# Softmax attention: two fp32r parts in 64-row tiles instead of six bf16 parts over the whole array

## The chip, the cores and the metric

The kernel is one program on one NeuronCore of a Trainium2 chip. The metric is the device time of one execution, in microseconds (us). Engines are named as in the profile: PE (TensorE matmul), PEld (its weight loads), DVE (VectorE), ACT (ScalarE), POOL (GpSimd), SP (the engine that issues the DMAs here).

## The reference

Two macaron blocks are computed on x of 2 x 2048 x 256 in fp32. Block 0 is a routed feed-forward, a causal linear attention and the feed-forward again; block 1 is an fp4-quantised feed-forward, a softmax attention and the quantised feed-forward again. The change touches only the softmax attention:

```python
b, n, _ = x.shape                       # 2, 2048
qkv = (x @ W_qkv.T).reshape(b, n, 16, 16).transpose(0, 2, 1, 3)
score = softmax(einsum('bhif,bhjf->bhij', qkv, qkv) / 4.0, axis=-1)
attn = einsum('bhij,bhjf->bihf', score, qkv)
out = attn.reshape(b, n, 256) @ W_o.T
```

Queries, keys and values are the same tensor: 16 heads of 16 features, 2048 x 2048 scores for each of 2 x 16 heads.

## The kernel before

The stage is `attn1()`. It works in 32 **units**: batch (2) x group of four heads (`NG` = 4) x block of 512 queries (`IC` = 4). A unit has two kinds of big work, both over 512 columns at a time (`GW` = 512):

- **maxima** ("max", 64 in a unit): 128 queries (stationary) against 512 keys (moving) of one head; DVE reduces the PSUM bank to one maximum for each query (line 1817). After 64 of them a small reduce makes the row maxima, PE transposes them ("extremes"), DVE and POOL split them into parts, and two DMAs bring them through DRAM into extra rows of the query operand, negated, so that the score product subtracts them by itself.
- **scores** ("score"): 128 keys (stationary) against 512 queries (moving), for each of 16 key tiles `jt` and four heads. ACT takes the exponential out of PSUM into `spr` (line 1775). Then "pv" multiplies the four heads' probabilities with the values (plain fp32, four 32-column tiles at once, line 1713) into one bank that accumulates over the 16 key tiles. "end" copies that bank to SBUF on ACT, "tail" transposes and divides by the row sums, "ao" and "wo" are the output projection and the residual.

The fp32 precision of the scores comes from **parts**: the projected values are split into three bf16 parts (ACT rounds, DVE takes the rest, POOL rounds and takes the rest again), stored in `q_parts` in DRAM, and gathered into stacks: `KS` holds the parts `KEY = [0,0,1,0,1,2]`, `QS` the parts `QRY = [0,1,0,2,1,0]`, 16 rows each, so that one product over 96 rows is the sum of six partial products; scores use 99 rows (three more for the maxima, against rows of ones in `KS`).

The order of the work is one written-out generator, `plan()`, which every engine walks through; each engine's instructions run in that order. The maxima run 80 ahead of the scores (a unit and a quarter). For each key tile before, the order is: max, two scores, max, two scores, max, pv, max. A pair of scores fills a two-bank PSUM tile that one 1024-wide exponential reads; there are two such tiles, three single banks (`spare`) shared by maxima and all other products in turn, and one bank for pv. The projection of the second batch ("norm", "turn", "parts", "value") and the output steps are put in between, one at a time. A stack for the next group of heads is loaded by SP a group ahead. An `Event` counts a semaphore; `made(what)` is the product being ready, `read(what)` its bank being free.

Of the kernel before, what the change touches and what calls it, by code (L numbers as in the profile page):

```python
# [6 lines left out]
F32 = mybir.dt.float32  # L7
# [7 lines left out]
P = 128  # L15
# [41 lines left out]
def build_program(nc, A):  # L57
# [21 lines left out]
    with ExitStack() as ctx:  # L79
# [1412 lines left out]
        def attn1():  # L1492
            with ExitStack() as scope:
                NPT = 6
                KR = NPT * DH
                KM = KR + 3
                HG = 4
                NG = NH // HG
# [5 lines left out]
                SPU = TB * HG // 2  # L1504
# [3 lines left out]
                PART, REST = ring(scope, "spart", [P, 3, GW], 2, BF16), sb("srest", [P, GW], scope=scope)  # L1508
# [4 lines left out]
                MR, MB = sb("smr", [NR, P], scope=scope), ring(scope, "smb", [NR, 3, P], 2, BF16)  # L1513
                RD, AO = ring(scope, "srd", [P, GT, HG], 2), sb("sao", [P, TB, D], scope=scope)
                AOT = ring(scope, "saoT", [P, D], 2)
                parts = nc.dram_tensor("q_parts", [3, D, L * nb], BF16).ap()
                maxima = nc.dram_tensor("row_maxima", [UNITS, 3, NR, P], BF16).ap()
# [7 lines left out]
                pm_in, pm_free = event("a1_pm_in"), [event(f"a1_pm_free{i}") for i in range(3)]  # L1525
                xn_ok, part0, rest_ok, part_ok = (event(f"a1_{n}") for n in ("xn", "part0", "rest", "part"))
                mx_ok, mb_ok, fill_ok = event("a1_mx"), event("a1_mb"), event("a1_fill")
# [13 lines left out]
                def output_steps(u):  # L1541
                    b, ic = u // (NG * IC), u % IC
                    for t in range(ic * GT, (ic + 1) * GT):
                        yield ("ao", b, t)
                        yield ("wo", b, t)

                def plan():
# [9 lines left out]
                    for u in range(UNITS):  # L1557
# [9 lines left out]
                        for h in range(2 * SPU):  # L1567
                            if m % MPU == 0 and m <= UNITS * MPU:
                                yield ("extremes", m // MPU - 1)
                            if m < UNITS * MPU:  # L1570
                                yield ("max", m)
                            m += 1
                            if h > 9 and h % 4 == 3:
                                yield from itertools.islice(aside, 1)
                            if h > 9 and h % 6 == 4:
                                yield from itertools.islice(put, 1)
                            if h % 4 < 2:
                                yield ("score", u * SPU + h // 4 * 2 + h % 4)
                            if h % 4 == 2 and u * TB + h // 4:
                                yield ("pv", u * TB + h // 4 - 1)  # L1580
                            if h == 2 and u:
                                yield ("end", u - 1)
                            if h == 8 and u:
                                yield ("tail", u - 1)
# [11 lines left out]
                def bank(key):  # L1596
                    return spare[use[key] % 3]

                def read(key):

                    return pm_free[use[key] % 3](use[key] // 3 + 1)
# [4 lines left out]
                with nc.Block() as block:  # L1606

                    @block.sync
                    def _(e):
                        for kind, *at in plan():  # L1610
                            if kind == "parts":
                                b, g, o = at
                                col = b * L + g * GW
                                e.wait_ge(*part_ok((b * IC + g) * KD + o + 1))
                                e.dma_start(parts[:, o * P:(o + 1) * P, col:col + GW].rearrange("s p n -> p s n"),
                                            PART[o][:]).then_inc(*part_out[o].up)
                            if kind == "stack":
# [6 lines left out]
                                for dst, which in ((KS[n % 2], KEY), (QS[n % 2], QRY)):  # L1624
                                    for j, part in enumerate(which):
                                        src = parts[part, g * HG * DH:(g + 1) * HG * DH, b * L:(b + 1) * L]
                                        e.dma_start(dst[j * DH:(j + 1) * DH], src.rearrange(
                                            "(h f) n -> f h n", f=DH)).then_inc(*stack_in[n % 2].up)
                            if kind == "extremes":
                                u = at[0]  # L1630
                                ic, n = u % IC, u // IC
                                e.wait_ge(*mb_ok(u + 1))
                                e.dma_start(maxima[u].rearrange("j r n -> r j n"), MB[u % 2][:]).then_inc(
                                    *max_in[u % 2].up)
                                e.wait_ge(*max_in[u % 2](2 * (u // 2) + 1))
                                e.dma_start(QS[n % 2][KR:KM, :, ic * GW:(ic + 1) * GW],
                                            maxima[u].rearrange("j (h i) n -> j h (i n)", h=HG)).then_inc(
                                    *max_in[u % 2].up)

                    @block.tensor  # L1640
                    def _(e):
                        def free(key):
                            k = use[key]
                            if k >= 3:
                                e.wait_ge(*pm_free[k % 3](k // 3))

                        for what in plan():
# [24 lines left out]
                            if kind == "max":  # L1672
                                u, r = divmod(at[0], MPU)
                                h, i, jc = r // (GT * IC), r // IC % GT, r % IC
                                n, q0 = u // IC, (u % IC * GT + i) * P
                                if r == 0 and u % IC == 0:
                                    e.wait_ge(*stack_in[n % 2]((n // 2 + 1) * 2 * NPT))
# [9 lines left out]
                            if kind == "score":  # L1687
                                q = at[0]
                                u, jt, hp = q // SPU, q % SPU // 2, q % 2
                                n, ic = u // IC, u % IC  # L1690
                                if q % SPU == 0:
                                    e.wait_ge(*max_in[u % 2](2 * (u // 2) + 2))
                                if q == 0:
                                    e.wait_ge(*fill_ok(2))
                                if q >= 2:
                                    e.wait_ge(*exp_ok(q - 1))
                                for i in range(2):
                                    m = e.matmul(st[q % 2][:, i, :], KS[n % 2][0:KM, 2 * hp + i, jt * P:(jt + 1) * P],  # L1698
                                                 QS[n % 2][0:KM, 2 * hp + i, ic * GW:(ic + 1) * GW], start=True,
                                                 stop=True)  # L1700
                                m.then_inc(*st_ok.up)
                            if kind == "pv":
# [7 lines left out]
                                e.wait_ge(*exp_ok(2 * j + 2))  # L1710
# [30 lines left out]
                    def _(e):  # L1741
                        e.wait_ge(*stats_ok(0))
                        std_of(e, 0, T).then_inc(*std_ok.up)
                        e.wait_ge(*fill_ok(2))
# [180 lines left out]
```

## Time and profile before

| | |
|---|---|
| median of 3 runs | 3826.54 us (3825.26 to 3828.68) |
| the profiled execution: its time | 3830.56 us |
| its span, first to last instruction | 3828.8 us |
| PE, PEld busy | 3580.0 us (94%), 2285.8 us (60%) |
| DVE, ACT, POOL busy | 2719.0 us (71%), 2054.4 us (54%), 663.9 us (17%) |
| mean granted TensorE clock | 0.971 |

The busy shares are means over stages that have different limits. The stage of the change lies between about 1840 and 3554 us of the span. A matmul's busy time is counted from its start to its modelled end, and matmuls overlap, so the distance between starts says more than the mean duration. In a timeline row the figures are start, duration, engine, line, operation, output and inputs, and a count; in square brackets the idle time of the engine ahead of it and what ended it.

### The profile page before, as it was taken

How to read it: one execution, taken by the hardware profiler on the slowest of the kernel's cores; microseconds unless marked ns; L12 is line 12 of the kernel's file. 1: busy time of each engine (PE TensorE's matmuls, PEld its weight loads, DVE VectorE, ACT ScalarE, POOL GpSimd, SP SyncE). 2: the span in 40 equal slices, each digit the busy share in tenths (PEclk: the TensorE clock that was granted, in tenths of full speed). 3: DMA queues.
4: the chain of work that ended last, by engine and by line, in shares of the span. 5: the costliest groups of instructions: out<-in, count | busy, mean ns of one | idle time of the engine just before them, and what ended most of it. 6: DMA issues, size and time to landing. Idle time of an engine off the chain costs nothing. (4 is left out here: it accounts for less than half of the span.)

```text
span 3828.8 us, 57043 instructions
## 1 busy us (share of the span) xinstructions
PE 3580.0 (94%) x22274; PEld 2285.8 (60%) x22274; DVE 2719.0 (71%) x4907; ACT 2054.4 (54%) x2806; POOL 663.9 (17%) x601
## 2 busy tenths in 40 slices
PE   6999998999799999799589999999999999999799
PEld 6888886777688888799313333333333333333698
DVE  4545544875444544799378788888888888884898
ACT  3444443433444444455226666666666666667555
POOL 4000002443400000455300000000000000000565
PEclk9999998999899999899869999999999999999899
DMA  3000001000200000000240120202020202000000
GB/s 115 1 1 1 1 1 40 2 2 1 71 1 1 1 1 1 1 1 1 50 50 10 30 31 5 30 9 27 1 34 1 34 2 34 1 1 1 6 18 23
DMA packets 39651, 61.42 MB, mean 16 GB/s; under 512 B 5284, under 2 KB 29912, under 8 KB 39384
## 3 DMA queue, kind: packets, MB, share of 16 engines
q1 hardware_dynamic: 39384, 57.78, 8.3%
q8 instruction: 177, 2.90, 0.3%
q14 instruction: 90, 0.74, 0.1%
HBM read 46.89 MB, written 10.88 MB: 15 GB/s over the span
## 5 line engine op out<-in xcount | busy, mean ns | idle before, releaser
L1817 DVE TENSOR_REDUCE smxp<-psum 128x1 f32<-128x512 f32 x2048 | 1281.7, 682 | 222.8 <-PE psum L1679 222.1
L1775 ACT ACTIVATE spr<-psum 128x1024 f32<-128x1024 f32 x1024 | 996.3, 1021 | 560.1 <-PE psum L1698 557.7
L1679 PE MATMUL psum<-sks,sqs 96*128 96x512 bf16 x2048 | 731.5, 392 | 34.3 <-DMA sqs<-q_parts 31.3
L1698 PE MATMUL psum<-sqs,sks 99*128 99x512 bf16 x2048 | 610.9, 380 | 0.4
L1713 PE MATMUL psum<-spr,sv 128*32 128x512 f32 x4096 | 546.4, 605 | 0.6 <-ACT spr L1775 0.6
L1679 PEld LDWEIGHTS psum<-sks,sqs 96*128 96x128 bf16 x2048 | 164.2, 97 | 614.0 <-issue 379.9
L1698 PEld LDWEIGHTS psum<-sqs,sks 99*128 99x128 bf16 x2048 | 199.7, 98 | 243.2 <-ACT spr L1775 15.2
L1886 POOL CAST smb<-smr 16x128 bf16<-16x128 f32 x32 | 9.0, 281 | 1356.4 <-DVE smr L1836 1356.4
L389 PE MATMUL psum<-w2hi_a,hsa_hi 128*128 128x256 f32 x768 | 217.3, 283 | 17.4 <-DVE hsa_lo L531 17.4
L389 PE MATMUL psum<-w2hi_b,hsb_hi 128*128 128x256 f32 x768 | 217.3, 283 | 10.5 <-DVE hsb_lo L531 10.5
L389 PE MATMUL psum<-w2lo_a,hsa_hi 128*128 128x256 f32 x768 | 217.7, 284 | 0.0
L389 PE MATMUL psum<-w2lo_b,hsb_hi 128*128 128x256 f32 x768 | 217.7, 284 | 0.0
L389 PE MATMUL psum<-w2hi_a,hsa_lo 128*128 128x256 f32 x768 | 217.4, 283 | 0.0
L389 PE MATMUL psum<-w2hi_b,hsb_lo 128*128 128x256 f32 x768 | 217.4, 283 | 0.0
L525 DVE TENSOR_TENSOR hidb<-psum,maskb 128x512 f32<-128x512 f32 x128 | 88.3, 690 | 173.8 <-PE psum L355 173.8
L531 DVE TENSOR_TENSOR hsa_lo<-hida,hsa_hi 128x512 fp32r<-128x512 f32 x192 | 148.0, 772 | 83.6 <-ACT hida L444 75.3
L531 DVE TENSOR_TENSOR hsb_lo<-hidb,hsb_hi 128x512 fp32r<-128x512 f32 x192 | 147.4, 769 | 83.6 <-ACT hidb L444 75.3
L1713 PEld LDWEIGHTS psum<-spr,sv 128*32 128x32 f32 x4096 | 80.7, 108 | 210.7 <-issue 193.3
L525 DVE TENSOR_TENSOR hida<-psum,maska 128x512 f32<-128x512 f32 x128 | 88.2, 689 | 157.5 <-PE psum L355 157.5
L447 ACT ACTIVATE hsb_hi<-hidb,b_b 128x512 fp32r<-128x512 f32 x128 | 92.6, 723 | 183.7 <-DVE hidb L525 183.7
L447 ACT ACTIVATE hsa_hi<-hida,b_a 128x512 fp32r<-128x512 f32 x128 | 92.6, 724 | 173.6 <-DVE hida L525 173.6
L389 PEld LDWEIGHTS psum<-w2hi_a,hsa_hi 128*128 128x128 f32 x768 | 146.0, 190 | 28.8 <-DVE hsa_lo L531 21.1
(350 smaller groups left out, 7259.3 us busy)
## 6 DMA issues: line engine op xcount, KB each, us to landing
sks<-q_parts SPq DMA_DIRECT2D x48, 256.0 KB, 8.8
sqs<-q_parts SPq DMA_DIRECT2D x48, 256.0 KB, 19.7
q_parts<-spart SPq DMA_DIRECT2D x16, 384.0 KB, 2.6
x<-in_L_attn_x_dram SPq DMA_DIRECT2D x8, 512.0 KB, 7.2
rawa<-in_L_ffn_w_dram SPq DMA_DIRECT2D x16, 256.0 KB
rawb<-in_L_ffn_w_dram SPq DMA_DIRECT2D x16, 256.0 KB
out_dram<-x SPq DMA_DIRECT2D x8, 512.0 KB, 2.9
rawa<-in_L_ffn_sw_dram SPq DMA_DIRECT2D x8, 256.0 KB
```

The source lines that it names most:

```text
L389: m = e.matmul(ops[:, i // 2, (i % 2) * D:(i % 2 + 1) * D], hs[u][:, i * P:(i + 1) * P], w2[v][:, ex, c, :], start=(s == 0 and i % 2 == 0 ...
L447: e.activation(hi[:], hid[:], ACT.Relu, bias=bias).then_inc(*sc.up())
L525: e.tensor_tensor(HB[n % 2][:], psum[:, j % 3, :], mask[:, s // C0 - 1, :], ALU.mult).then_inc(*masked.up)
L531: e.tensor_tensor(lo[:], HB[n % 2][:], hi[:].bitcast(F32), ALU.subtract).then_inc(*low_ok.up)
L1679: e.matmul(bank(what), QS[n % 2][0:KR, h, q0:q0 + P], KS[n % 2][0:KR, h, jc * GW:(jc + 1) * GW], start=True, stop=True).then_inc(*pm_in.up)
L1698: m = e.matmul(st[q % 2][:, i, :], KS[n % 2][0:KM, 2 * hp + i, jt * P:(jt + 1) * P], QS[n % 2][0:KM, 2 * hp + i, ic * GW:(ic + 1) * GW], s ...
L1713: m = e.matmul(po[32 * hq:32 * hq + VW, :], VB[b][:, jt, c0:c0 + VW], PR[j % 2][:, hq, :], start=(jt == 0), stop=(jt == TB - 1), tile_posi ...
L1775: e.activation(PR[j % 2][:, 2 * hp:2 * hp + 2, :], st[hp], ACT.Exp, scale=float(DH) ** -0.5).then_inc(*exp_ok.up)
L1817: e.tensor_reduce(MXP[u % 2][:, r // IC, r % IC:r % IC + 1], bank(what), AX.X, ALU.max).then_inc(*pm_free[use[what] % 3].up)
L1886: e.tensor_copy(MB[u % 2][:, 1, :], MR[:]).then_inc(*pl.up())
```

## The change

- Two fp32r parts take the place of three bf16 parts. A stack is then 3 x 16 = 48 rows (`KEY = [0,0,1]`, `QRY = [0,1,0]`), 50 rows with the maxima (in two parts). POOL's casts and subtractions go; DVE writes the second part itself.
- Two heads share the 128 partitions: one in rows 0 to 49, one in rows 64 to 113. Each max and score product is a 64-row tile (`tile_position=(64 * a, 0)`), with `a` alternating 0, 1. Columns, outputs and the number of products stay as they are.
- The PSUM banks are dealt anew: four single banks for the maxima and the small products, three single banks for scores, one for pv. Each score has its own 512-wide exponential (2048 instead of 1024).
- The order for each key tile is `m s0 s1 m s2 v m s3 m`: max, scores 0 and 1, max, score 2, pv of the key tile before, max, score 3, max. A score waits for the exponential three scores back.
- The rows of ones in `KS` are written by eight small DMAs from a 2 x 64 tile, instead of two POOL memsets over 3 x 8192 elements.
- The parts go through DRAM in fp32 (512 KB for each store instead of 384 KB); a stack is still 12 DMAs of 256 KB, six to each of `KS` and `QS`. The maxima come back in two DMAs instead of one.

```diff
-                NPT = 6
+                NPT = 3
                 KR = NPT * DH
-                KM = KR + 3
+                KM = KR + 2
+                HALF = 64
-                KEY = [0, 0, 1, 0, 1, 2]
-                QRY = [0, 1, 0, 2, 1, 0]
+                KEY = [0, 0, 1]
+                QRY = [0, 1, 0]
+                ORDER = ("m s0 s1 m s2 v m s3 m").split()
-                KS, QS = ring(scope, "sks", [P, HG, L], 2, BF16), ring(scope, "sqs", [P, HG, L], 2, BF16)
+                KS, QS = ring(scope, "sks", [P, NPR, L], 2, F32R), ring(scope, "sqs", [P, NPR, L], 2, F32R)
-                st = (psum[:, 0:2, :], psum[:, 2:4, :])
-                po = psum[:, 6, :]
-                spare = (psum[:, 4, :], psum[:, 5, :], psum[:, 7, :])
+                spare = [psum[:, i, :] for i in range(4)]
+                st = [psum[:, 4 + i, :] for i in range(3)]
+                po = psum[:, 7, :]
...
-                        for h in range(2 * SPU):
+                        for jt in range(TB):
+                            j = u * TB + jt
+                            for step in ORDER:
+                                if step[0] == "s":
+                                    yield ("score", j, int(step[1]))
+                                if step == "v" and j:
+                                    yield ("pv", j - 1)
+                                if step == "m":
+                                    if m % MPU == 0 and m <= UNITS * MPU:
+                                        yield ("extremes", m // MPU - 1)
+                                    if m < UNITS * MPU:
+                                        yield ("max", m)
+                                    m += 1
...
                             if kind == "max":
-                                e.matmul(bank(what), QS[n % 2][0:KR, h, q0:q0 + P],
-                                         KS[n % 2][0:KR, h, jc * GW:(jc + 1) * GW], start=True,
-                                         stop=True).then_inc(*pm_in.up)
+                                rows = slice(HALF * a, HALF * a + KR)
+                                e.matmul(bank(what), QS[n % 2][rows, pr, q0:q0 + P],
+                                         KS[n % 2][rows, pr, jc * GW:(jc + 1) * GW], start=True, stop=True,
+                                         tile_position=(HALF * a, 0)).then_inc(*pm_in.up)
...
                             if kind == "score":
-                                if q >= 2:
-                                    e.wait_ge(*exp_ok(q - 1))
-                                for i in range(2):
-                                    m = e.matmul(st[q % 2][:, i, :], KS[n % 2][0:KM, 2 * hp + i, jt * P:(jt + 1) * P],
-                                                 QS[n % 2][0:KM, 2 * hp + i, ic * GW:(ic + 1) * GW], start=True,
-                                                 stop=True)
-                                m.then_inc(*st_ok.up)
+                                if s >= 3:
+                                    e.wait_ge(*exp_ok(s - 2))
+                                e.matmul(st[s % 3], KS[n % 2][rows, pr, jt * P:(jt + 1) * P],
+                                         QS[n % 2][rows, pr, ic * GW:(ic + 1) * GW], start=True, stop=True,
+                                         tile_position=(HALF * a, 0)).then_inc(*st_ok.up)
...
-                                e.wait_ge(*exp_ok(2 * j + 2))
+                                e.wait_ge(*exp_ok((j + 1) * HG))
...
-                        e.memset(KS[0][KR:KM], 1.0).then_inc(*fill_ok.up)
-                        e.wait_ge(*fill_ok(1))
-                        e.memset(KS[1][KR:KM], 1.0).then_inc(*fill_ok.up)
-                        e.wait_ge(*fill_ok(2))
+                        e.tensor_scalar(ones[:], ident[0:2, 0:1].to_broadcast([2, HALF]), 0.0, 1.0, ALU.mult,
+                                        ALU.add).then_inc(*fill_ok.up)
```

## Rows read from the trace of the kernel before

**Rows 1.** Groups: line, engine, shapes, count | busy us, mean ns | idle before.

```profile
L1817 DVE TENSOR_REDUCE smxp<-psum 128x1 f32<-128x512 f32 x2048 | 1281.7, 682 | 222.8 <-PE psum L1679 222.1
L1775 ACT ACTIVATE spr<-psum 128x1024 f32<-128x1024 f32 x1024 | 996.3, 1021 | 560.1 <-PE psum L1698 557.7
L1713 PE MATMUL psum<-spr,sv 128*32 128x512 f32 x4096 | 546.4, 605 | 0.6 <-ACT spr L1775 0.6
L870 PEld LDWEIGHTS psum<-aqe,aqT 32*128 32x128 f32 x512 | 45.2, 189 | 16.2 <-issue 8.7 <-POOL aqe L1178 1.2
```

**Rows 2.** Windows: length, busy PE, PEld, DVE, ACT, POOL, then PEclk, DMA share, GB/s.

```profile
1930.00:1978.50 48.50, 47.06 (x82) 8.32 (x81) 47.65 (x82) 0.00 (x0) 0.70 (x2) 0.50 0.10 14
1978.50:3493.30 1514.80, 1483.21 (x8282) 480.31 (x8282) 1299.49 (x2213) 997.90 (x1078) 34.94 (x76) 1.00 0.13 18
```

**Rows 3.** Timeline of one key tile in the steady state.

```profile
2502.55 0.11 PEld L1679 LDWEIGHTS psum<-sks,sqs 96*128 96x128 bf16 x2 [0.84 <-issue]
...
2502.99 2.48 DVE L1817 TENSOR_REDUCE smxp<-psum 128x1 f32<-128x512 f32 x4 [0.35 <-PE psum L1679]
...
2503.63 1.94 ACT L1775 ACTIVATE spr<-psum 128x1024 f32<-128x1024 f32 x2 [0.90 <-PE psum L1698]
...
2504.39 0.16 PEld L1713 LDWEIGHTS psum<-spr,sv 128*32 128x32 f32 x8 [0.42 <-issue]
...
2505.39 0.11 PEld L1679 LDWEIGHTS psum<-sks,sqs 96*128 96x128 bf16 x2 [0.84 <-issue]
```

**Rows 4.** Timeline where DVE alone sets the pace, with the first extremes.

```profile
1964.40 4.26 DVE L1817 TENSOR_REDUCE smxp<-psum 128x1 f32<-128x512 f32 x7
...
1969.91 0.67 DVE L1817 TENSOR_REDUCE smxp<-psum 128x1 f32<-128x512 f32 x1
```

**Rows 5.** Timeline of PE's weight loads over a key tile with extremes.

```profile
2015.95 0.10 PEld L1679 LDWEIGHTS psum<-sks,sqs 96*128 96x128 bf16 x1 [0.84 <-issue]
...
2020.10 0.11 PEld L1679 LDWEIGHTS psum<-sks,sqs 96*128 96x128 bf16 x2 [0.84 <-issue]
```

**Rows 6.** Timeline of PE: fp32r products over 512 columns in block 0's attention.

```profile
701.12 0.40 PE L760 MATMUL psum<-wqkv0T_hi,axT_lo 128*128 128x512 f32 x1
701.35 0.40 PE L760 MATMUL psum<-wqkv0T_hi,axT_hi 128*128 128x512 f32 x1
```

**Rows 7.** Timeline: plain fp32 products, first in 32-row tiles, then over the whole array.

```profile
702.85 0.52 PEld L870 LDWEIGHTS psum<-aqe,aqT 32*128 32x128 f32 x6
702.85 0.70 PE L870 MATMUL psum<-aqe,aqT 32*128 32x256 f32 x4
...
1890.30 3.70 PE L1662 MATMUL psum<-sxT,wqkv1T 128*128 128x512 f32 x8 [0.47 <-ACT sxT L1753]
```

**Rows 8.** Timeline of the last unit, which has scores and no maxima.

```profile
3501.47 3.91 ACT L1775 ACTIVATE spr<-psum 128x1024 f32<-128x1024 f32 x4 [0.27 <-PE psum L1698]
3501.79 0.16 PEld L1713 LDWEIGHTS psum<-spr,sv 128*32 128x32 f32 x8 [0.42 <-issue]
...
3503.46 0.11 PEld L1698 LDWEIGHTS psum<-sqs,sks 99*128 99x128 bf16 x2 [0.56 <-ACT spr L1775]
3504.00 0.16 PEld L1713 LDWEIGHTS psum<-spr,sv 128*32 128x32 f32 x8 [0.42 <-issue]
...
3504.99 0.11 PEld L1698 LDWEIGHTS psum<-sqs,sks 99*128 99x128 bf16 x2 [0.84 <-ACT spr L1775]
...
3505.26 0.60 ACT L1782 ACTIVATE sot<-psum 128x512 f32<-128x512 f32 x1
```

**Rows 9.** Timeline of the stage's start, up to the first maxima.

```profile
1841.75 6.92 POOL L1868 MEMSET sks<- 3x8192 bf16 x1
...
1855.72 0.39 ACT L1753 ACTIVATE sxT<-psum 128x256 f32<-128x256 f32 x1 [13.85 <-POOL sks L1870]
...
1895.65 0.69 DVE L1810 TENSOR_TENSOR srest<-psum,spart 128x512 f32<-128x512 f32 x1 [2.02 <-POOL spart L1879]
...
1929.66 0.13 PEld L1679 LDWEIGHTS psum<-sks,sqs 96*128 96x128 bf16 x2 [31.67 <-DMA sqs<-q_parts]
```

More of the change, by code:

```diff
@@ L1566, in plan @@
                         put = output_steps(u - 1) if u and (u - 1) // IC % NG == NG - 1 else iter(())
-                        for h in range(2 * SPU):
[L1568 to L1573, printed above, removed]
+                        for jt in range(TB):
[11 more added lines that the diff above has]
+                                    m += 1
+                            if jt == 0 and u:
+                                yield ("end", u - 1)
+                            if jt == 1 and u:
+                                yield ("tail", u - 1)
+                            if jt > 0:
                                 yield from itertools.islice(aside, 1)
-                            if h > 9 and h % 6 == 4:
+                            if jt > 1:
                                 yield from itertools.islice(put, 1)
[L1577 to L1584, printed above, removed]
                         yield from put
@@ L1609, in _ @@
                     def _(e):
-                        for kind, *at in plan():
+                        e.wait_ge(*fill_ok(1))
+                        for ks in KS:
+                            for pr in range(NPR):
+                                for i in range(2):
+                                    e.dma_start(ks[HALF * i + KR:HALF * i + KM, pr, :].bitcast(F32).rearrange("p (c n) -> p c n", n=HALF),
+                                                ones[:].bitcast(F32).unsqueeze(1).to_broadcast([2, L // HALF, HALF])).then_inc(*ones_in.up)
+                        for what in plan():
+                            kind, *at = what
                             if kind == "parts":
@@ L1625, in _ @@
                                     for j, part in enumerate(which):
-                                        src = parts[part, g * HG * DH:(g + 1) * HG * DH, b * L:(b + 1) * L]
-                                        e.dma_start(dst[j * DH:(j + 1) * DH], src.rearrange(
-                                            "(h f) n -> f h n", f=DH)).then_inc(*stack_in[n % 2].up)
+                                        src = parts[part, g * HG * DH:(g + 1) * HG * DH, b * L:(b + 1) * L].rearrange(
+                                            "(r i f) n -> i f r n", i=2, f=DH)
+                                        for i in range(2):
+                                            row = HALF * i + j * DH
+                                            e.dma_start(dst[row:row + DH].bitcast(F32), src[i]).then_inc(*stack_in[n % 2].up)
                             if kind == "extremes":
@@ L1754, in _ @@
                                              bank(what)[:, 0:D].rearrange("p (k n) -> p k n", k=KD),
-                                             ACT.Copy).then_inc(*pm_free[use[what] % 3].up)
+                                             ACT.Copy).then_inc(*pm_free[use[what] % 4].up)
                             if kind == "parts":
@@ L1816, in _ @@
                                     e.wait_ge(*mx_ok(u - 1))
-                                e.tensor_reduce(MXP[u % 2][:, r // IC, r % IC:r % IC + 1], bank(what), AX.X,
-                                                ALU.max).then_inc(*pm_free[use[what] % 3].up)
+                                out = MXP[u % 2][:].rearrange("p (r a i) c -> p r i c a", r=NPR, a=2)
+                                e.tensor_reduce(out[:, r // (2 * GT * IC), r // (2 * IC) % GT, r // 2 % IC, r % 2:r % 2 + 1],
+                                                bank(what), AX.X, ALU.max).then_inc(*pm_free[use[what] % 4].up)
                                 if r == MPU - 1:
-                                    for k in range(3):
+                                    for k in range(4):
                                         e.wait_ge(*read(("max", at[0] - k)))
```

120 lines of the change are left out of this document (52 added, 68 removed).

## The prediction

> **What bounds the kernel now.** I read the windows first. The stage has a stretch with maxima alone and one of 1514.8 us with maxima and scores together [rows 2]. In the second, PE's busy time is 1483 us, but durations overlap there, so it doesn't tell the bound; DVE is busy 1299 us and ACT 998 us, so neither is full. The groups say who waits for whom: DVE's reduces wait 222 us for the max products, ACT's exponentials 558 us for the scores, pv waits for nobody [rows 1]. Both consumers wait for PE. The timeline of one key tile confirms it: the tile repeats every 2505.39 - 2502.55 = 2.84 us. Of this, eight 512-column products (four maxima, four scores) take 2504.39 - 2502.55 = 1.84 us, 0.22 us each with about 0.1 us ahead of pv, and pv takes 1.00 us. PE is never idle; DVE has 2.48 us of reduces and waits 0.35 us, ACT has 1.94 us [rows 3].
>
> By the plan, 2048 - 80 = 1968 maxima lie in this stretch, 4 to a key tile, so 492 key tiles. 492 x 2.835 = 1395 us, and 120 us are left for all else: the extremes (a key tile with them takes 2020.10 - 2015.95 = 4.15 us, 1.31 more, so 31 x 1.31 = 41 us [rows 5]), the second batch's projection, tails and output products.
>
> **What a key tile costs after: PE.** The products are as many and as wide. Two things change. First the rate: fp32r products over 512 columns start 0.235 us apart [rows 6] against 0.22 for bf16. Second, neighbours in different row halves can run at once. No row shows this for fp32r in 64-row tiles. The nearest is block 0's attention: plain fp32 products of 256 columns in two 32-row tiles in turn start about 0.11 us apart: four in 0.70 us, the last of them 0.38 long [rows 7] (a plain fp32 record of 512 columns lasts 0.605 [rows 1], one of 256 by half the columns 0.22 less). Over the whole array the same kind needs (3.70 - 0.60)/7 = 0.44 us for 512 columns [rows 7], so 0.22 for 256. Two row tiles do halve the time there, and the weight loads of 128 fp32 columns keep up: each lasts 0.19 us [rows 1], but six take 0.52, so they start (0.52 - 0.19)/5 = 0.07 us apart [rows 7]. In the new order every product finds a neighbour of the other half: after pv, m2|s3, m3|m0, s0|s1, m1|s2. Four slots of 0.235, plus the 0.1 ahead of pv and pv itself, make 2.04 us. Bounds: all pairs, 2.04; no pairs, 8 x 0.235 + 1.10 = 2.98. I take all pairs, since the one row with row tiles shows the full factor.
>
> The Trainium skill (TensorEngine Tiling, Key Properties) says that changing the tiling mode, not just the tile, drains TensorE. This speaks for a cost at each switch between 64-row products and pv; the rows show such a cost already, since pv is column-tiled before too, about 0.1 us ahead of it and 0.15 inside its 1.00, and the count of switches stays. By the page the sum is then unchanged.
>
> **DVE.** Its reduce is untouched. Back to back, reduces start (4.26 - 0.68)/6 = 0.597 us apart [rows 4], 2.39 us for four. **ACT.** A 1024-wide exponential takes 1.02 us and a 512-wide copy 0.60 [rows 1, 8], so 512 columns cost 0.42 and the rest is fixed; two in a row take 1.94 us, so starts are 0.92 apart; at half the width 0.50, and four make 2.0 us. Neither PE nor ACT nor, at 2.39, DVE needs the old 2.84.
>
> **The chain between PE and ACT.** The new order closes a loop. Score 2 of a key tile reuses the bank of score 3 of the tile before, so it waits for that exponential (e3), as does the pv behind it. Score 3 is issued only after this pv, and e3 follows it. One turn is one key tile:
> - e3's end to the weight load of s2: the second of four exponentials, which start (3.91 - 1.02)/3 = 0.96 apart, ends at 3501.47 + 0.96 + 1.02 = 3503.45, load at 3503.46: 0.01 [rows 8].
> - s2 to pv: 0.54 for two bf16 scores [rows 8], less one at 0.22, plus 0.02 for the rate and 0.08 for an fp32 load of 0.19 [rows 1] instead of 0.11: 0.42.
> - pv to the next load: 0.99 [rows 8].
> - m2 and s3, to the start of e3: a max's load to its reader took 0.44 [rows 3]; plus 0.10 as above, plus 0.06 because s3's load comes second: 0.60.
> - e3: 0.60 [rows 8].
>
> Sum 2.62 us. It is more than PE's 2.04, ACT's 2.0 and DVE's 2.39, so this wait, new with the change, takes the place of the old bound. Lower bound 2.50 (loads hidden, s3 not behind m2), upper 2.75 (m2 and s3 one after the other, 0.14 more). I take 2.62. The maxima's four banks hold 4 x 0.6 us of work for DVE and bridge pv.
>
> **The rest of that stretch.** Extremes: PE stands until DVE has read the last max and the small reduce, then 1969.91 - (1964.40 + 4.26) = 1.25 us go by until its next max, with the small reduce and the copies in them [rows 4]; with m3 read later in the tile I get 1.6 instead of 1.31 us, +10 us over 31 units. The PE work put in between (projection, output products) now falls partly into PE's idle 0.4 us per tile: some 75 such steps that held the path, at most 0.45 each, so up to -34, and DVE's own part of the output steps takes some back: -28. The 120 become 102. Stretch: 492 x 2.62 + 102 = 1391 us, **-124**.
>
> **The stage's start.** Two POOL memsets of 6.9 us hold back ACT's first copy: it waits 13.85 us and starts at 1855.72 [rows 9]. Without them POOL is done at 1841.75 plus a tiny operation; norm and transposes are then the chain and the copy starts near 1843.3: -12. In the projection DVE waits 2.02 us for POOL once a block [rows 9], and PE's value products wait behind it about 1.0: -4 over four blocks; the last parts reach DRAM without POOL's two operations (about the 2 us that DVE waited for them) and without part of that wait: -3; stores are a third larger: +0.6. The stack's load, 31 us ahead of the first max [rows 9], has the same number of DMAs and bytes: 0, with 5 less and 10 more as bounds since its pieces are longer. The eight DMAs of ones are needed only at the first score, 80 maxima (48 us) later: hidden; if not, a few us once. The extremes' second DMA has 16 maxima (9.6 us) of cover. Sum **-18**. The 48.5 us with maxima alone [rows 2] are DVE's and stay.
>
> **The last unit** has no maxima: a key tile from pv to pv takes 3504.00 - 3501.79 = 2.2 us [rows 8]; the loop without m2 is 2.5: 16 x 0.3 = **+5**.
>
> Sum: -124 - 18 + 5 = -137 us on the profiled execution (time 3830.6, span 3828.8), which lies 4 us over the median. From the median 3826.5: **3690 us**.
>
> **The rivals.**
> - *DVE becomes the bound* (the loop closes faster, or its load and latency terms are smaller): 2.39 a tile, 492 x -0.445 = -219, start -18, last unit +3, the 120 stay: 3592. For it: five small terms make up the loop, and each is a bound from bf16 rows. Against: DVE must then never wait. The Trainium skill (TensorEngine Tiling, PSUM Bottleneck) says that tiling speeds up TensorE but not the reading of PSUM; by that rule alone this rival is the answer, and the loop is what I set against it. Chance 0.17.
> - *Pairs overlap only in part* (a pair in about 0.35 us, or waits for banks break pairs up): 2.8 a tile, with the other terms about 3780. Chance 0.10.
> - *No pairs, slower:* fp32r row tiles run one after another. PE again is the bound with 2.98 a tile: 492 x +0.145 = +71, start -18, last unit +7, and the 120 stay: 3886. It decides from the point where a tile takes 2.86, a pair over 0.44 us. For it: no row has fp32r in row tiles. Against: rows 7. Chance 0.13.
> - *The clock:* with maxima alone PE was granted 0.50, the 1.2 GHz level [rows 2], though PE had work every 0.6 us, and 1.00 only with scores. If the new, half-filled products kept it at 0.50, pv would take about 1.9 and a tile about 3.9: some 4330. Against: at the low level PE would be full. Chance 0.05.
>
> The forecast has the remaining 0.55, its own range 3630 to 3750 (2.50 to 2.75, start and load). The first rival with it makes 0.72; adding most of the partial overlaps gives 0.80 for 3590 to 3800. Faster by over 0.2%, about what a measurement of this kernel tells from no change: 0.80; within: 0.03; slower: 0.17.
>
> **What would show it.** Right: starts of m2 and s3 under 0.12 us apart; a tile of about 2.6 us with PE waiting for ACT at s2; ACT idle ahead of e3 only; DVE's idle about 0.2 us a tile; the first copy near 1843. Wrong: 64-row products 0.235 us apart even with alternating halves; PE waiting for DVE at the maxima (then 2.4); a clock of 0.50 beyond the first scores; fp32r weight loads that stand between products of one half.

## The result, and the profile after

The changed kernel takes 3767.07 us (median of 4, 3751.38 to 3784.17) against 3825.9 us (3821.71 to 3828.68): ratio 0.9851, 95% interval [0.9828, 0.9873]. It is faster by 59 us; 136 were forecast. The profiled execution took 3781.05 us (span 3779.3, mean granted clock 0.953), 49.5 less than that of before.

The groups of the page after, to be held against [rows 1]:

```profile
L1836 DVE TENSOR_REDUCE smxp<-psum 128x1 f32<-128x512 f32 x2048 | 1276.3, 682 | 175.3 <-PE psum L1701 168.8
L1796 ACT ACTIVATE spr<-psum 128x512 f32<-128x512 f32 x2048 | 1082.3, 599 | 470.9 <-PE psum L1720 462.2
L1720 PEld LDWEIGHTS psum<-sqs,sks 50*128 50x128 f32 x2048 | 323.1, 194 | 200.9 <-ACT spr L1796 170.0
```

New is the size of the wait in the last line: the scores' weight loads wait 170 us for exponentials, 15 before. PE, for which both others wait, now itself waits for ACT. The timeline of one steady key tile after, the answer to [rows 3]:

```profile
2503.24 0.18 PEld L1701 LDWEIGHTS psum<-sks,sqs 48*128 48x128 f32 x1 [0.84 <-issue]
2503.25 0.49 PE L1701 MATMUL psum<-sks,sqs 48*128 48x512 f32 x1
2503.25 0.49 PE L1720 MATMUL psum<-sqs,sks 50*128 50x512 f32 x1
2503.58 0.40 PE L1701 MATMUL psum<-sks,sqs 48*128 48x512 f32 x2
2503.78 2.48 DVE L1836 TENSOR_REDUCE smxp<-psum 128x1 f32<-128x512 f32 x4 [0.15 <-PE psum L1701]
2503.81 2.06 ACT L1796 ACTIVATE spr<-psum 128x512 f32<-128x512 f32 x4 [0.57 <-PE psum L1720]
2503.81 0.41 PE L1720 MATMUL psum<-sqs,sks 50*128 50x512 f32 x2
2504.46 0.18 PEld L1720 LDWEIGHTS psum<-sqs,sks 50*128 50x128 f32 x1 [0.45 <-ACT spr L1796]
2504.89 0.16 PEld L1734 LDWEIGHTS psum<-spr,sv 128*32 128x32 f32 x8 [0.24 <-ACT spr L1796]
2505.88 0.18 PEld L1701 LDWEIGHTS psum<-sks,sqs 48*128 48x128 f32 x1 [0.84 <-issue]
```

The max of one half and the score of the other start together (both 2503.25); the next two pairs follow at 2503.58 and 2503.81. The fourth does not come about: max 1 goes alone, since score 2 has to wait. The tile repeats every 2505.88 - 2503.24 = 2.64 us. The predicted loop can be read off: load of score 2 (s2) at 2504.46, 0.43 to pv, 0.99 to the next load, and from 2503.24 another 0.57 to the first exponential (2503.81) and 0.65 from there to the load of s2.

The windows of the stage's last two stretches after (maxima with scores; last unit), with busy time and count of PE, PEld, DVE, ACT and POOL, granted clock, DMA share and GB/s; the first answers to the long stretch of [rows 2]:

```profile
1957.40:3422.80 1465.40, 1422.23 (x8275) 572.46 (x8273) 1294.21 (x2211) 1074.05 (x2058) 0.00 (x0) 0.96 0.13 19
3422.80:3492.70 69.90, 65.63 (x272) 21.03 (x272) 5.62 (x18) 43.99 (x85) 0.00 (x0) 0.73 0.00 1
```

The granted clock is 0.96 and 0.73, where before it was 1.00 but for 3.5 us [rows 2]. The profile's clock records hold 121 us at 0.50 (1.2 GHz) between the first pv and the last max, and 37.5 us more behind it. One such place, the timeline behind the extremes of a unit, and the windows ahead of it, in it and after it:

```profile
2380.28 0.09 PEld L1708 LDWEIGHTS psum<-ident,smx 128*16 128x16 f32 x1 [1.83 <-DVE smx L1843]
2382.47 0.29 PEld L1701 LDWEIGHTS psum<-sks,sqs 48*128 48x128 f32 x1 [0.94 <-issue]
2384.71 1.93 PE L1734 MATMUL psum<-spr,sv 128*32 128x512 f32 x8
2388.81 0.20 PEld L1734 LDWEIGHTS psum<-spr,sv 128*32 128x32 f32 x8 [0.44 <-issue]
```

```profile
2372.00:2378.00 6.00, 5.97 (x40) 2.07 (x37) 5.69 (x11) 4.87 (x10) 0.00 (x0) 1.00 0.21 27
2383.00:2392.00 9.00, 9.00 (x38) 3.91 (x35) 5.46 (x9) 4.81 (x9) 0.00 (x0) 0.50 0.01 2
2394.00:2404.00 10.00, 9.96 (x64) 4.22 (x66) 9.25 (x17) 7.97 (x16) 0.00 (x0) 1.00 0.01 2
```

PE's loads wait 1.83 us for DVE's small reduce. Two microseconds later the clock is at 0.50, and a key tile takes 4.10 us (2388.81 - 2384.71) with PE full; the fall lasts some 10 us, then it is 1.00 again.

Where the 49.5 us are, stretch by stretch (marks: first norm, first max read, first pv, the pv 491 key tiles later, which is near the last max, and the last pv):

| stretch | before | after | difference | predicted |
|---|---|---|---|---|
| ahead of the stage (not touched) | 1842.3 | 1836.3 | -6.0 | 0 |
| first norm to first max | 88.0 | 69.3 | -18.7 | -18 |
| first max to first pv | 54.6 | 51.8 | -2.8 | 0 |
| 491 key tiles with maxima | 1509.8 | 1467.1 | -42.7 | -124 |
| last 20 key tiles | 47.1 | 68.2 | +21.1 | +5 |
| behind | | | -0.4 | 0 |

The first row is no gain of the change: in the kept traces this untouched part ends anywhere between 1836.3 and 1844.6 us.

### The profile page after: what moved, and what is told of

It is laid out like the page before. It is cut to its first block and busy times, and to the rows that moved or that the text cites. A ratio compares the mean times of both kernels' runs of the same rounds, so it can differ in the third digit from the quotient of the medians.

```text
span 3779.3 us, 57424 instructions
## 1 busy us (share of the span) xinstructions
PE 3535.4 (94%) x22274; PEld 2399.2 (63%) x22274; DVE 2698.2 (71%) x4907; ACT 2136.2 (57%) x3830; POOL 600.5 (16%) x504
## 5 line engine op out<-in xcount | busy, mean ns | idle before, releaser
L1796 ACT ACTIVATE spr<-psum 128x512 f32<-128x512 f32 x2048 | 1082.3, 599 | 470.9 <-PE psum L1720 462.2
L1720 PE MATMUL psum<-sqs,sks 50*128 50x512 f32 x2048 | 754.6, 470 | 6.4 <-ACT spr L1796 3.1
L1701 PE MATMUL psum<-sks,sqs 48*128 48x512 f32 x2048 | 677.1, 457 | 29.5 <-DMA sqs<-q_parts 29.1
L1701 PEld LDWEIGHTS psum<-sks,sqs 48*128 48x128 f32 x2048 | 292.3, 198 | 538.7 <-issue 461.3
L1734 PE MATMUL psum<-spr,sv 128*32 128x512 f32 x4096 | 576.8, 636 | 1.8 <-ACT spr L1796 0.7
L1720 PEld LDWEIGHTS psum<-sqs,sks 50*128 50x128 f32 x2048 | 323.1, 194 | 200.9 <-ACT spr L1796 170.0
```

The lines of the kernel that those rows point to most:

```text
L1701: e.matmul(bank(what), QS[n % 2][rows, pr, q0:q0 + P], KS[n % 2][rows, pr, jc * GW:(jc + 1) * GW], start=True, stop=True, tile_position=(H ...
L1720: e.matmul(st[s % 3], KS[n % 2][rows, pr, jt * P:(jt + 1) * P], QS[n % 2][rows, pr, ic * GW:(ic + 1) * GW], start=True, stop=True, tile_po ...
L1734: m = e.matmul(po[32 * hq:32 * hq + VW, :], VB[b][:, jt, c0:c0 + VW], PR[j % 2][:, hq, :], start=(jt == 0), stop=(jt == TB - 1), tile_posi ...
L1796: e.activation(PR[j % 2][:, hq, :], st[s % 3], ACT.Exp, scale=float(DH) ** -0.5).then_inc(*exp_ok.up)
```

## The experiments

Three theories stood against each other. The pause theory: the pause at the extremes makes the granted clock fall, and this with the stall ate the gain. The pairs theory: the loop isn't the bound, pairs overlap in part or DVE sets the tile. The half-rows theory: products that fill half the rows can't hold the clock, pause or not.

**late_extremes**: the extremes are put four maxima later, when DVE has long read their input. Nothing is left out.

```diff
+                LATE = 4
-                                    if m % MPU == 0 and m <= UNITS * MPU:
+                                    if m % MPU == LATE and m <= UNITS * MPU + LATE:
                                         yield ("extremes", m // MPU - 1)
```

> The changed kernel, with the extremes four maxima later in the order, so that PE need not stand until DVE has read the last maximum of a unit. Theory (the granted clock falls because PE stands idle about 1.8 us at each extremes): no fall of the clock to 0.50 between the first and the last maximum; a key tile with extremes takes 3.0 us instead of 4.24, 31 x 1.2 = 38 us, and the falls were worth about 60 us more in the profiled run, so 3670 to 3690 us. Rival (the clock falls because the products fill half the rows, whatever the gaps): the falls stay, only the 38 us go, 3725 to 3735 us.

3694.62 us (3691.98 to 3714.01) against 3827.97: ratio 0.9666 [0.9639, 0.9694], a little above the range expected. Its windows of the two last stretches, and one line of the timeline at an extremes:

```profile
1961.30:3345.30 1384.00, 1380.13 (x8281) 557.10 (x8284) 1287.55 (x2212) 1071.38 (x2060) 0.00 (x0) 1.00 0.14 20
3345.30:3400.40 55.10, 50.62 (x266) 17.10 (x258) 5.59 (x17) 43.11 (x84) 0.00 (x0) 0.97 0.01 1
```

```profile
2242.40 0.09 PEld L1709 LDWEIGHTS psum<-ident,smx 128*16 128x16 f32 x1 [0.37 <-issue]
```

The transpose waits for nobody now, the clock stays at 1.00, a tile with extremes takes 2.76 instead of 4.24 us. The 491 tiles take 83.3 us less. Of these, 27 x 1.48 and four times 0.5 (units 2 to 5, where projection steps hide part of the pause) make 42 us of stall, which leaves 41 for the clock. That holds for the profiled run of 3691.98 us; the one of 3714.01 had a mean clock of 0.965 against its 0.971, so falls may have come back there. The products are the same half-filled pairs, so for pairs the half-rows theory (pause or not) falls.

**before_late_extremes**: the same edit in the kernel before.

> The kernel before with the same single edit. PE stands about 1.4 us at each extremes there too and the clock never falls, so if the clock is the difference this gives only the stall: 31 x 1.1 = 34 us, 3790 us. If the stall is needed for DVE to catch up, nothing.

3803.59 us (3795.85 to 3804.52), ratio 0.993 [0.9915, 0.9944]: -24, less than expected. There the pause cost only its own stall (the 491 tiles take 28.5 us less); the rest of what late_extremes won comes from the change.

**one_half**: every max and score product uses rows 0 to 49, so none has a neighbour in the other half.

```diff
-                                rows = slice(HALF * a, HALF * a + KM)
+                                rows = slice(0, KM)
...
-                                         tile_position=(HALF * a, 0)).then_inc(*st_ok.up)
+                                         tile_position=(0, 0)).then_inc(*st_ok.up)
```

> The changed kernel with every max and score product in rows 0 to 49 (the heads in rows 64 to 113 are left out and the others computed twice), so no two can overlap. Theory (two row halves run at once): a key tile takes 2.98 us or a little more instead of 2.64, PE never waits, about 3900 us. Rival (halves never overlapped, the tile was 2.64 for another reason): no change. For the clock: PE has no pause but the extremes here with the same half-filled products; if half filling is what lowers the clock, it falls here as often or more, if the pauses do, it falls seldom or never.

4984.03 us (one run). Windows of three stretches:

```profile
1960.00:2100.00 140.00, 138.96 (x397) 64.74 (x397) 67.36 (x105) 56.19 (x101) 0.00 (x0) 0.50 0.11 14
2373.00:2500.00 127.00, 124.69 (x651) 62.97 (x650) 101.67 (x171) 87.16 (x162) 0.00 (x0) 1.00 0.22 26
2520.00:4614.00 2094.00, 2072.16 (x5855) 970.09 (x5854) 997.84 (x1580) 817.38 (x1447) 0.00 (x0) 0.50 0.05 7
```

At 1.00 a tile took 3.06 us, near the 2.98 of the rival "no pairs". But in the last window the clock is 0.50 for 2094 us, with PE busy for 2072 of them, and a tile takes 5.57. The expectation missed this. The long fall begins 2.3 us behind the transpose of an extremes. Half-filled products one at a time did not bring the clock back, though PE was busy 99% of the time. In this stretch it rose once, at 2107 us, while the second batch's full-array projection products were mixed in (the last at 2304); the full-array output products in the last window did not raise it.

**serial_full**: the products are as many and as wide, over 112 rows of the whole array, one after another.

```diff
-                                rows = slice(HALF * a, HALF * a + KR)
+                                rows = slice(0, 112)
...
-                                         tile_position=(HALF * a, 0)).then_inc(*pm_in.up)
+                                         KS[n % 2][rows, pr, jc * GW:(jc + 1) * GW], start=True, stop=True).then_inc(*pm_in.up)
```

> The changed kernel with every max and score product over 112 rows of the whole array in place of a 64-row tile. It leaves out the separation of the two heads, the maxima (the ones are zeros) and the scale of the exponent. As in the run with one half, nothing can overlap, but the rows are filled. Theory (a stretch of half-filled products does not bring the clock back to 1.00): a tile of about 3.0 us as there, at a clock of 1.00 from the first scores on, about 3900 us. Rival (serial fp32r products as such keep the clock low): again near 5000 us.

3922.42 us (one run). The window of the stretch, and PE's timeline of one tile:

```profile
1972.00:3575.00 1603.00, 1571.10 (x8275) 829.42 (x8273) 1296.78 (x2211) 1099.07 (x2058) 0.00 (x0) 1.00 0.12 17
```

```profile
2309.99 0.50 PE L1701 MATMUL psum<-sks,sqs 112*128 112x512 f32 x1
2313.03 0.50 PE L1701 MATMUL psum<-sks,sqs 112*128 112x512 f32 x1
```

PE's weight load at an extremes:

```profile
2387.02 0.09 PEld L1707 LDWEIGHTS psum<-ident,smx 128*16 128x16 f32 x1 [1.60 <-DVE smx L1841]
```

3.04 us a tile: without pairs two fp32r parts are slower than six bf16 parts (2.84). A pause at the extremes is still there and the clock is 1.00 all the same. But it is shorter, 1.60 us against 1.83 (in the kernel before it is 1.33, without falls too). So pauses of this size between whole-array products brought no fall; whether the rows or the 0.23 us make the difference, this run does not separate.

**half_exp**: each exponential covers 256 of its 512 columns; the other probabilities are constants.

```diff
-                                e.activation(PR[j % 2][:, hq, :], st[s % 3], ACT.Exp,
+                                e.activation(PR[j % 2][:, hq, 0:GW // 2], st[s % 3][:, 0:GW // 2], ACT.Exp,
```

> The changed kernel with each exponential over 256 of its 512 columns (the other half of the probabilities is a constant 1, so half of the queries are left out). Theory (the loop score 2, pv, score 3, its exponential sets the key tile): 0.21 us less in e3, a tile of 2.43 us, about 490 x 0.21 = 100 us less than the changed kernel. Rival (DVE or PE sets the tile): 2.64 stays and only ACT has more idle time.

3722.31 us (one run). The timeline of one tile:

```profile
2270.13 0.18 PEld L1701 LDWEIGHTS psum<-sks,sqs 48*128 48x128 f32 x1 [0.84 <-issue]
2270.70 1.43 ACT L1796 ACTIVATE spr<-psum 128x256 f32<-128x256 f32 x4 [0.99 <-PE psum L1720]
2271.13 0.18 PEld L1720 LDWEIGHTS psum<-sqs,sks 50*128 50x128 f32 x1 [0.17 <-ACT spr L1796]
2272.55 0.18 PEld L1701 LDWEIGHTS psum<-sks,sqs 48*128 48x128 f32 x1 [0.84 <-issue]
```

2.42 us a tile, 0.22 less, though PE and DVE do the same work. The exponential is in the loop, as the prediction had it; a tile bound by PE or by DVE would not have moved. (At 2.42 DVE's reduces run without a break, so DVE may now limit the tile too.) The clock falls stay (117.8 us).

**late_s3_first**: late_extremes, and score 3 right behind pv.

```diff
-                ORDER = ("m s0 s1 m s2 v m s3 m").split()
+                ORDER = ("m s0 s1 m s2 v s3 m m").split()
```

> The kernel with late extremes, and score 3 as the first product behind pv instead of the second (order m s0 s1 m s2 v s3 m m). Theory (the loop sets the key tile): e3 starts up to 0.06 us sooner, a tile of 2.60 to 2.64 us, so 0 to 20 us less than with late extremes alone. Rival (the maxima set the pace): max 2 comes later by as much and the tile grows to 2.68 or more.

3678.4 us (3671.63 to 3683.65) against 3827.35: ratio **0.9609 [0.9595, 0.9623]**, the best version. Timeline, one turn of the loop:

```profile
2270.69 0.18 PEld L1721 LDWEIGHTS psum<-sqs,sks 50*128 50x128 f32 x1 [0.42 <-ACT spr L1797]
2273.28 0.18 PEld L1721 LDWEIGHTS psum<-sqs,sks 50*128 50x128 f32 x1 [0.41 <-ACT spr L1797]
```

2.59 us from s2 to s2 (2.60 to 2.61 over the stretch).

**late_two_steps**: late_extremes, and the second batch's projection steps put in two at a time, every other key tile.

```diff
-                            if jt > 0:
-                                yield from itertools.islice(aside, 1)
+                            if jt % 2 == 1:
+                                yield from itertools.islice(aside, 2)
```

> The kernel with late extremes, and the steps of the second batch's projection put in two at a time in every other key tile. With one value product a tile grows from 2.64 to 3.63: 0.86 of product, less 0.44 of PE's idle time before score 2, so 0.57 is left for going from 64-row tiles to the whole array and back. Theory (that is paid once for each interruption): a tile with two value products takes 2.64 + 2 x 0.86 + 0.57 - 0.44 = 4.49 us. Rival (it is paid for each product): 2.64 + 2 x 0.86 + 2 x 0.57 - 0.44 = 5.06 us.

3732.13 us (one run). First the timeline at one "parts" step in the kernel before, then in the changed kernel, then this kernel's, at a transpose and at two parts steps in a row:

```profile
2061.49 0.39 PE L1679 MATMUL psum<-sks,sqs 96*128 96x512 bf16 x1
2061.71 1.88 PE L1662 MATMUL psum<-sxT,wqkv1T 128*128 128x512 f32 x4
2063.43 0.38 PE L1679 MATMUL psum<-sks,sqs 96*128 96x512 bf16 x1
```


```profile
2030.68 0.40 PE L1701 MATMUL psum<-sks,sqs 48*128 48x512 f32 x1
2031.01 1.98 PE L1683 MATMUL psum<-sxT,wqkv1T 128*128 128x512 f32 x4
2032.92 0.49 PE L1701 MATMUL psum<-sks,sqs 48*128 48x512 f32 x1
```

```profile
2031.12 0.20 PEld L1677 LDWEIGHTS psum<-ident,sxn 128*128 128x128 f32 x2 [1.90 <-DVE sxn L124]
...
2094.20 0.40 PE L1702 MATMUL psum<-sks,sqs 48*128 48x512 f32 x1
2094.53 3.70 PE L1684 MATMUL psum<-sxT,wqkv1T 128*128 128x512 f32 x8
2098.16 0.50 PE L1702 MATMUL psum<-sks,sqs 48*128 48x512 f32 x1
```

From the max ahead of the step to the one behind it: 2.24 us with one step, 3.96 with two, and 1.94 in the kernel before. A step is thus 1.72 us of work, and an interruption costs 2.24 - 1.72 - 0.24 = 0.28 us beside the max's own 0.24; before it cost nothing (1.94 - 1.72 = 0.22, the max's own time). It also splits a pair of maxima, 0.24 more. It is paid once per interruption, as expected: two value products together made a tile of 4.49. The kernel is slower than late_extremes all the same: a norm and its transpose now stand side by side, PE waits for DVE there (16 times, 1.73 to 2.16 us), and clock falls are back (46.4 us). All four begin 1.0 to 1.8 us behind such a wait, the first of them 1.8 us behind the one shown. So a pause of PE can bring a fall wherever it comes from.

**memset_back**: POOL's two memsets come back ahead of the ones.

```diff
+                        for ks in KS:
+                            e.memset(ks[0:3].bitcast(BF16)[:, :, 0:2 * L], 1.0).then_inc(*pl.up())
+                            e.wait_ge(*pl.now())
```

> The changed kernel with two POOL memsets over 3 x 8192 bf16 elements put back ahead of the ones (into rows that the stacks overwrite later). The stage's start was 18.7 us shorter with the change. Theory (12 of them were the memsets): the first maximum comes 10 to 14 us later, counted from the stage's first norm. Rival (the start is bound by DVE's norms and the transposes): no change.

3829.86 us (one run). The timeline of POOL, DVE and ACT:

```profile
1835.77 13.92 POOL L1886 MEMSET sks<- 3x8192 bf16 x2
1836.31 13.85 DVE L124 TENSOR_SCALAR sxn<-x,mv,rstd 128x256 f32<-128x256 f32 x3
1850.05 0.39 ACT L1774 ACTIVATE sxT<-psum 128x256 f32<-128x256 f32 x1 [14.16 <-POOL sones L1888]
```

From first norm to first max: 82.2 instead of 69.3 us, 12.9 for the memsets (12 were predicted). The prediction let ACT's copy wait for POOL; what the memsets hold up is DVE ahead of it. Its first two normalisations last 6.52 and 7.09 us beside the memsets, three 13.85 together, where in the changed kernel (first row of the fence on the start, further down) two take 0.74. The other 36 us of this run are chiefly clock: 148 us at 0.50 in the long stretch and 99 behind it.

**The last three runs** were to price the clock apart from the stall, since moving the extremes removes both, and to see which pauses bring falls. **after_again** is the changed kernel itself. In **fill_full** PE fills the pause with products that nobody reads, and **fill_half** does so with half-filled ones:

```diff
                                 u = at[0]
-                                e.wait_ge(*mx_ok(u + 1))
                                 free(what)
+                                for i in range(8):
+                                    e.matmul(bank(what)[:, 0:P], ident[:], ident[:], start=True, stop=True)
+                                e.wait_ge(*mx_ok(u + 1))
```

```diff
+                                for i in range(6):
+                                    rows = slice(0, KR)
+                                    e.matmul(bank(what), KS[u // IC % 2][rows, 0, 0:P], KS[u // IC % 2][rows, 0, 0:GW],
+                                             start=True, stop=True, tile_position=(0, 0))
```

> The changed kernel itself, unaltered, for a second profile. If which pauses lead to a fall of the granted clock is a matter of chance, the time at 0.50 between the first pv and the last maximum differs from the 121 us of the first profile and falls lie in other units; if the plan of the work decides it, they lie in the same units. A tile is 2.64 us either way; time 3750 to 3785.

> Ahead of each wait for the small reduce, PE does eight products it doesn't need (128 columns of the identity, over the whole array, 0.18 us each, 1.44 us in all) into the bank that the transpose is to use anyway. The pause of 1.83 us becomes one of about 0.4; the tile with extremes stays about 4.2 to 4.3 us. If PE's pause brings the falls of the clock, they go (51 us in the profiled run): 3725 to 3745. If falls come from the paired half-filled products whatever PE does in the pause, they stay: 3755 to 3790. This separates the price of the stall from that of the clock, which moving the extremes removed together.

> As the run with eight full products, but with six fp32r products of 48 rows in the upper half alone, 0.235 us each, 1.41 us in all. If any work in the pause will do, the falls go here too, 3725 to 3745. If half-filled products count for less, as in the run with all products in one half, the falls stay or grow: 3755 to 3800.

| kernel | time | ratio | at 0.50, long stretch | tile with extremes |
|---|---|---|---|---|
| after_again | 3777.41 (3757.87 to 3797.71) | 0.9859 [0.9804, 0.9914] | 104.1 | 4.24 |
| fill_full | 3750.59 (3748.25 to 3757.77) | 0.9792 [0.9775, 0.981] | 2.4 | 4.64 |
| fill_half | 3739.82 (3736.45 to 3748.34) | 0.9769 [0.9754, 0.9785] | 7.4 | 4.24 |

fill_half, its timeline at an extremes and its windows of the last two stretches:

```profile
2381.39 1.32 PE L1709 MATMUL psum<-sks 48*128 48x512 f32 x5
2382.95 0.09 PEld L1712 LDWEIGHTS psum<-ident,smx 128*16 128x16 f32 x1 [0.68 <-DVE smx L1847]
```

```profile
1959.60:3389.30 1429.70, 1420.09 (x8459) 583.80 (x8458) 1293.50 (x2210) 1070.73 (x2058) 0.00 (x0) 1.00 0.14 19
3389.30:3445.10 55.80, 51.00 (x273) 17.64 (x271) 6.28 (x19) 43.84 (x86) 0.00 (x0) 1.00 0.01 1
```

The chain is as late as before (the transpose at the same distance behind the maxima, the tile still 4.24), PE does work that is thrown away, and the kernel is some 38 us faster by the medians. The pause theory is shown: what costs, beside the stall, is PE's idle time ahead of the extremes, through the clock. Half-filled work does as well as full; the eight full products overrun the pause (tile 4.64; 31 x 0.4 = 12 us, about the 11 between the two medians), so fill_full lies above the range expected.

Which pauses bring a fall changes from run to run. The starts of the falls in us behind the extremes of their unit, from the clock records (without the last unit, and of half_exp units 11 to 25 alone). Three more, one in after and two in after_again, begin 0.0 to 0.3 us ahead of a transpose, within the pause itself:

```
after        u6 1.4  u7 0.2  u9 1.9  u10 1.9  u11 1.8  u12 1.7  u14 1.0  u15 1.6  u16 1.0  u17 1.4  u27 1.9  u28 1.8  u29 1.8
after_again  u6 1.5  u14 0.7  u17 0.2  u20 1.9  u21 1.9  u22 1.8  u23 1.7  u30 0.9
half_exp     u11 0.0  u12 0.3  u13 0.4  u14 0.6  u15 0.8  u16 1.0  u19 1.8  u20 0.1  u21 0.3  u22 0.5  u23 0.6  u24 0.8  u25 1.0
```

They often come in runs of neighbouring units whose distance drifts steadily, with units without any between, though each unit from 6 on has the same pause; units 2 to 5, where it is under 0.9 us, have no fall. So it seems to matter where in time the pause lies against something that isn't tied to the kernel. That is read off these lists, not tested. It agrees with the spread of times: the changed kernel's runs have 3751.38 us at a mean clock of 0.964 and 3797.71 at 0.947.

## Why the prediction was wrong, point by point

**Right in mechanism and size.** Pairs overlap fully (starts 0.01 us apart, a pair every 0.24), three of them a tile instead of the four predicted; serial_full shows what it would be without, 3.04. The loop over the exponential sets the tile: 2.64 against 2.62. Its terms came out at 0.43, 0.99, 0.57 and 0.65 against 0.42, 0.99, 0.60 and 0.61, and half_exp moved the tile by about what one shorter exponential gives (0.60 to 0.38 us). A tile with extremes takes 4.24, predicted 1.6 + 2.62. The two rivals on pairs fell; so did the DVE rival: DVE still waits in each tile (0.15 us here).

The Trainium skill (TensorEngine Tiling (Array Packing), PSUM Bottleneck) says that tiling speeds up TensorE but not the reading of PSUM. The trace agrees in so far as the tile stayed above DVE's 2.48; the bound itself was a loop through ACT.

The start is right too, -18.7 for -18, read in the changed kernel's timeline:

```profile
1836.26 0.74 DVE L124 TENSOR_SCALAR sxn<-x,mv,rstd 128x256 f32<-128x256 f32 x2
1837.51 0.75 ACT L1774 ACTIVATE sxT<-psum 128x256 f32<-128x256 f32 x2 [1.67 <-PE psum L1676]
1904.77 0.50 PEld L1701 LDWEIGHTS psum<-sks,sqs 48*128 48x128 f32 x4 [29.48 <-DMA sqs<-q_parts]
```

ACT's first copy comes at 1837.51, 1.3 us behind the first norm (13.4 before, [rows 9]); the wait for the stack is 29.5 us against 31.7 before.

**The step that failed: the clock as a rival of its own, all or nothing, at 0.05.** The text set against it that PE would be full at the low level. one_half refutes this as a reason: PE was full for 2094 us and the clock stayed at 0.50. And it needn't stay down to cost: the falls are short and come behind the extremes, whose pause the prediction had itself lengthened to 1.6 us. It priced that stall and not what PE's idle time does to the clock. Price by fill_half: its 491 tiles take 1431.5 us, 36 less than the changed kernel's, though four of them lost 1.2 us each to the filler: 40 us for 114 us less at 0.50. In the last 20 tiles the clock costs about 14 more (68.2 against 54.0 in fill_half).

**The second step: "the count of switches stays", and with it the -28 for inserted steps.** Of the 81 us by which the long stretch missed, the tile's 0.02 makes 491 x 0.02 = 10, the clock some 40, and the rest, 31, is this. Counted tile by tile in the profiled runs, the inserted steps hold 77 us before and 81 after (in late_extremes, which has hardly any fall), where 28 less than before were forecast. A value or output product made its tile 0.86 us longer before, its work alone, and makes it 0.99 longer after, though PE's idle 0.44 us does absorb work, as said. What eats that up is the interruption of the 64-row products by a full-array step: 0.28 us, and 0.24 for the pair that it splits. Before there was neither, since maxima, scores and projection were all in the whole array. It is the tiling and not fp32r: the same product makes a tile 0.85 longer in serial_full, with fp32r over the whole array, and 1.25 in one_half, with 64-row products and no pair to split. The prediction cited the Trainium skill (TensorEngine Tiling (Array Packing), Key Properties) for the drain at a change of mode and counted only the switches around pv; the trace agrees with the page, at 0.28 us for out and back, and the count was wrong.

**The last unit:** +21 for +5: 14 is clock, 7 the tiles. The plain tile is 2.6 instead of 2.5. And the 2.2 read for before is one tile: from pv to pv they take 1.97 to 2.92 there, 2.4 in the mean, and in fill_half 2.7 in the mean, both with the output steps.

Sum of the profiled run: -18.7 - 2.8 - 42.7 + 21.1 - 6.4 = -49.5. Without the falls (40 + 14) it would be -103, which fill_half comes near (its profiled run is 91.6 under that of before, with 5 us lost to the filler). That late_extremes, at 3694.62, lands beside the forecast of 3690 is chance: the 42 us of stall that the forecast kept are gone, and the inserted steps (32) and the tile (10) cost as much more than it said.

What stays open: what decides, pause by pause, whether the clock falls, and whether serial_full keeps it because its products fill the rows or because its pause is 0.23 us shorter.

## What to carry to other kernels

When PE stops being the bound, its idle time appears in one place or another, and it can cost twice: once as the stall, once as the clock behind it. Look for the longest single pause of PE, not the sum, and either move its cause (four maxima later gave -72 us here) or give PE something to do in it. When products move into row tiles, count each step of another tiling mode that is put between them, and put such steps together, but not two that wait for each other.

## What the runs showed of the hardware that was not expected

- Products in rows 0 to 49 alone, one at a time, kept the granted clock at 0.50 for 2094 us with PE busy 99% of it; over 112 rows, one at a time, it stayed at 1.00 for 1603 us.
- Work whose result is thrown away made the kernel faster, by some 38 us.
- An fp32r product of 50 rows and 512 columns and its neighbour in the other half start 0.01 us apart and take 0.24 us together, as much as one alone.
- DVE's normalisations lasted as long as the POOL memsets of 6.9 us beside them: 6.52 and 7.09 us, against 0.41 without them.
- An interruption of 64-row products by full-array ones cost 0.28 us in all, whether one step or two stood in it; between whole-array products it cost nothing.
